# Four reorderings in a fused cross-attention and feed-forward kernel: low-rank stacks, last reciprocals, first operands, turned values

## The reference, cut to what matters

```python
x = x + xattn0(layernorm(x), ctx)      # 32 query heads of 32, 8 groups of keys and values
#   q = ln @ w_q.T ; k = ctx @ w_k.T ; v = ctx @ w_v.T ; softmax(mask(q k)) v ; @ w_out.T
x = x + ffn0(layernorm(x))
#   base = ln @ W_base.T + b_base
#   e = ln @ enc.T (rank 40) ; decoded = e @ (coefs * mask).T for 3 experts, inverse real FFT, sum, * 0.5
x = x + quantised_matmul(layernorm(x), ctx)
x = x + mixing(x)                      # 4 streams, Sinkhorn with 50 iterations
```

## Time and profile before

| | |
|---|---|
| median of 3 runs | 1081.86 us (1080.81 to 1082.34) |
| profiled execution | 1082.79 us, its span 1081.0 us |
| PE busy | 1036.2 us, 96% |
| DVE busy | 873.5 us, 81% |
| ACT busy | 663.4 us, 61% |
| mean granted TensorE clock | 0.983 of full |

### The profile page before, as it was taken

One profiled execution on the slowest core, in us unless ns is written; L12 is line 12 of the kernel. 1 busy time (PEld: TensorE's weight loads), 2 busy tenths in 40 slices (PEclk: granted clock), 3 DMA queues, 4 the chain that ended last, 5 costly groups with the idle time before them and its releaser, 6 DMA issues. The chain is left out here.

```text
span 1081.0 us, 20198 instructions
## 1 busy us (share of the span) xinstructions
PE 1036.2 (96%) x7174; PEld 782.8 (72%) x7174; DVE 873.5 (81%) x1880; ACT 663.4 (61%) x1126; POOL 93.0 (9%) x85
## 2 busy tenths in 40 slices
PE   8999999999999999999999999998999999956978
PEld 7878888777777777777777777765888887534647
DVE  5763544799999999999999999955774795879998
ACT  4332320498999889899989989942222114635837
POOL 0221011200000000000000000000003112400000
PEclk9999999999999999999999999999999999987989
DMA  8458779831133323212332321166315000000003
GB/s 330 176 162 293 258 262 277 316 116 43 39 74 73 73 68 73 52 35 63 73 73 68 73 59 33 38 240 233 118 59 170 0 0 1 1 1 1 1 1 155
DMA packets 55568, 112.95 MB, mean 104 GB/s; under 512 B 7724, under 2 KB 21164, under 8 KB 55388
## 3 DMA queue, kind: packets, MB, share of 16 engines
q1 hardware_dynamic: 55402, 112.10, 33.7%
q10 hardware_dynamic: 50, 0.16, 0.0%
q0 software_dynamic: 64, 0.00, 0.0%
HBM read 83.99 MB, written 27.26 MB: 103 GB/s over the span
## 5 line engine op out<-in xcount | busy, mean ns | idle before, releaser
L886 DVE CUSTOM_DVE_ANT_0 XS<-b_psS,b_mbias 128x1024 f32<-128x1024 f32 x256 | 310.9, 1215 | 0.9 <-PE b_psS L766 0.7
L841 ACT ACTIVATE XS<-XS,b_mins 128x1024 f32<-128x1024 f32 x256 | 295.8, 1155 | 10.1 <-DVE b_mins L886 9.5
L799 PEld LDWEIGHTS b_psT<-ident,XS 128*128 128x128 f32 x2048 | 230.0, 140 | 65.7 <-issue 47.6
L799 PE MATMUL b_psT<-ident,XS 128*128 128x128 f32 x2048 | 271.9, 276 | 1.7 <-ACT b_PT L849 1.7
L895 DVE COPY b_PT<-b_psT 128x512 f32<-128x512 f32 x256 | 176.8, 691 | 26.8 <-PE b_psT L799 24.9
L849 ACT COPY b_PT<-b_psT 128x512 f32<-128x512 f32 x256 | 149.5, 584 | 38.8 <-PE b_psT L799 30.8
L766 PE MATMUL b_psS<-XTh 128*128 128x512 f32 x512 | 155.9, 422 | 0.7 <-PEq L115 0.6
L780 PE MATMUL b_psO<-b_PT,XTh 128*32 128x256 f32 x1984 | 132.8, 385 | 0.0
L766 PEld LDWEIGHTS b_psS<-XTh 128*128 128x128 f32 x512 | 85.1, 189 | 18.5 <-DVE b_mins L886 7.7
L780 PEld LDWEIGHTS b_psO<-b_PT,XTh 128*32 128x32 f32 x1984 | 51.8, 109 | 42.1 <-issue 20.8
L416 ACT ACTIVATE a_oh<-a_psM 128x512 fp32r<-128x512 f32 x24 | 14.2, 595 | 81.4 <-PE a_psM L335 50.4
(11 more groups left out here) (268 smaller groups left out, 1616.6 us busy)
## 6 DMA issues: line engine op xcount, KB each, us to landing
XS<-in_ctx SPq DMA_DIRECT2D x16, 512.0 KB, 5.8
XTh<-QHd SPq DMA_DIRECT2D x32, 256.0 KB, 4.4
XTh<-QLd SPq DMA_DIRECT2D x32, 256.0 KB, 5.1
XS<-in_ctx_turned SPq DMA_DIRECT2D x8, 512.0 KB, 10.9
XS<-in_x SPq DMA_DIRECT2D x8, 512.0 KB, 11.4
a_wst<-in_L_xattn_w_q SPq DMA_DIRECT2D x8, 512.0 KB, 5.9
a_xn<-in_ctx_turned SPq DMA_DIRECT2D x8, 512.0 KB, 4.2
QHd<-a_oh SPq DMA_DIRECT2D x16, 256.0 KB, 5.5
```

What stands on the lines that cost most here:

```text
L799: last_t = pe.transpose(psT[:, kt, :], Pr[:, k % PR, kt * P:(kt + 1) * P], ident[:])
L841: act.activation(Pr[:, k % PR, :], Sc[:, k % 4, :], ACT.Exp, bias=mins[:, k % 4:k % 4 + 1], scale=-1.0, accum_out=sums[:, u, j:j + 1]).the ...
L886: dve.tensor_tensor_reduce(out=Sc[:, k % 4, :], in0=psS[:, k % 2, :], in1=mbias[:, qt, :], scale=1.0, scalar=3.4e38, op0=ALU.add, op1=ALU.min,
```

## The change

Four places are edited.

1. Stage A: the transposes of the values (`turn_v(0)`, `turn_v(1)`) go behind the query products 8 and 9. The first query product waits for four token tiles, the second for all eight. On DVE `keep_values` and `keep_product` of products 6 and 7 go behind the next weights' low part.
2. The seam between stages B and C: the last unit's reciprocals (DVE) and their widening (POOL) are issued in stage C, behind the barrier.
3. The first operands of stage C: the attention tile 0 is split in two parts, the first 256 columns (`FIRST` is 2 blocks of 128) ahead of the weights, the rest behind the second weight tile. The first two steps of `first_layer` wait for the first part alone.
4. The stacks of T: ACT makes T32 and its high part ahead of `std` and `attention_hi(3)`; DVE's low part goes ahead of `attention_lo(3)`; the DMA of the low rows moves from ACT's queue to SP's, ahead of the two next attention loads. DVE waits for the rest of `x` in step 2 and not in step 1.

```diff
@@ stage_a, tensor @@
-            turn_v(0)
+            pe.wait_ge(x_split, NT // 2)
             for m in range(M_Q, M_V1):
-                if m == M_Q:
-                    pe.wait_ge(x_split, NT // 2)
-                elif m == M_Q + 1:
-                    turn_v(1)
+                if m == M_Q + 1:
                     pe.wait_ge(x_split, NT)
                 product(m, XTh, XTl)
+                if m < M_Q + KVT:
+                    turn_v(m - M_Q)
@@ stage_a, vector @@
-            keep_values(0)
-            keep_product(2 * V0 + 2)
-            keep_product(2 * V0 + 3)
             for t in range(KT):
                 weights_lo(Q0 + 1 + t)
+                if t == 0:
+                    keep_values(0)
+                    keep_product(2 * V0 + 2)
+                    keep_product(2 * V0 + 3)
                 store_lo(M_Q + 2 * t)
+                ctx_lo(KT + t)
+                if t:
+                    quantise(t)
+                store_lo(M_Q + 2 * t + 1)
                 if t == 0:
                     keep_values(1)
-                ctx_lo(KT + t)
-                quantise(t)
-                store_lo(M_Q + 2 * t + 1)
+                    quantise(0)
@@ LastUnit @@
+    def spread_out(self, pool, u):
+        n = QT * HPG
+        pool.tensor_tensor(self.wide.rearrange("p t (h d) -> p (t h) d", d=DH),
+                           self.rec[:, u, :].unsqueeze(2).to_broadcast([P, n, DH]),
+                           self.one.unsqueeze(2).to_broadcast([P, n, DH]), ALU.mult).then_inc(self.rec_ready, 1)
+
+    def widen(self, pool):
+        pool.wait_ge(self.rec_ready, 2 * BG - 1)
+        self.spread_out(pool, 1)
@@ stage_b, vector @@
-            dve.wait_ge(probs, BG * STEPS)
-            end.reciprocals(dve)
@@ stage_b, gpsimd @@
-            with pool.Fori(0, BG // 2) as it:
+            with pool.Fori(0, BG // 2 - 1) as it:
                 for u in range(2):
                     widen(it, u)
+            widen(BG // 2 - 1, 0)
@@ stage_cd, sync @@
-            sp.wait_ge(wo_split, KT)
+            sp.wait_ge(wo_split, KT + 1)
...
+            sp.wait_ge(T_split, 1)
+            sp.dma_start(TS[stack_rows(1), :].bitcast(F32), lo_rows[0:RANK, 0, :].bitcast(F32)).then_inc(stacks_in, 16)
@@ stage_cd, tensor, first_layer @@
-                pe.wait_ge(op_split, 1)
                 for k in range(KT):
-                    pe.wait_ge(wo_split, k + 1)
+                    pe.wait_ge(wo_split, k + 2)
+                    if k == FIRST:
+                        pe.wait_ge(op_split, 1)
@@ stage_cd, scalar @@
-            attention_hi(0)
+            act.wait_ge(ao_in[0], 16)
+            act.activation(Lh[:, 0, 0:FIRST, :], src[:, 0, 0:FIRST * P].rearrange("p (k n) -> p k n", k=FIRST), ACT.Copy
+                           ).then_inc(wo_hi, 1)
             for k in range(KT):
                 act.wait_ge(wo_in[k // (KT // 2)], 16)
                 act.activation(WOh[:, k, :], XR[:, k, :], ACT.Copy).then_inc(wo_hi, 1)
+                if k == FIRST - 1:
+                    act.activation(Lh[:, 0, FIRST:, :], src[:, 0, FIRST * P:].rearrange("p (k n) -> p k n", k=KT - FIRST),
+                                   ACT.Copy).then_inc(op_hi, 1)
...
-                if i + 1 < NT:
+                if i + 1 < NT and i != T_TILE + 1:
                     attention_hi(i + 1)
...
-                std((i - 1) * 3 + 2)
-                if i == T_TILE + 1:
+                if i != T_TILE + 1:
+                    std((i - 1) * 3 + 2)
+                else:
                     act.wait_ge(T_done, 1)
...
-                    act.wait_ge(T_split, 1)
-                    act.dma_start(TS[stack_rows(1), :].bitcast(F32), lo_rows[0:RANK, 0, :].bitcast(F32)
-                                  ).then_inc(stacks_in, 16)
+                    std((i - 1) * 3 + 2)
+                    attention_hi(i + 1)
@@ stage_cd, vector @@
-            attention_lo(0)
+            end.reciprocals(dve)
+            lo_part(Ll[:, 0, 0:FIRST, :].rearrange("p k n -> p (k n)"), src[:, 0, 0:FIRST * P],
+                    Lh[:, 0, 0:FIRST, :].rearrange("p k n -> p (k n)"), wo_hi, 1, wo_split)
             for k in range(KT):
-                lo_part(WOl[:, k, :], XR[:, k, :], WOh[:, k, :], wo_hi, k + 1, wo_split)
+                lo_part(WOl[:, k, :], XR[:, k, :], WOh[:, k, :], wo_hi, k + 2, wo_split)
+                if k == FIRST - 1:
+                    lo_part(Ll[:, 0, FIRST:, :].rearrange("p k n -> p (k n)"), src[:, 0, FIRST * P:],
+                            Lh[:, 0, FIRST:, :].rearrange("p k n -> p (k n)"), op_hi, 1, op_split)
...
+                if i == 2:
+                    dve.wait_ge(x_in[1], 16)
                 residual(i - 1, (i - 1) % 2, 0)
-                if i == 1:
-                    dve.wait_ge(x_in[1], 16)
+                if i == T_TILE + 1:
+                    lo_part(lo_rows[0:RANK, 0, :], T32, hi_rows[0:RANK, 0, :], T_step, 3, T_split)
                 if i + 1 < NT:
                     attention_lo(i + 1)
...
-                    lo_part(lo_rows[0:RANK, 0, :], T32, hi_rows[0:RANK, 0, :], T_step, 3, T_split)
@@ stage_cd, gpsimd @@
+            end.widen(pool)
             pool.wait_ge(end.weighed, BG * 2)
```

More of the change, by code:

```diff
@@ L631, in __init__, with take @@
         self.stored = [sem(f"b_stored{u}") for u in range(2)]
-    def take(self, PT, Vs, rec, wide, sums, Os, AOs, psO):
-        self.PT, self.Vs, self.rec, self.wide, self.sums, self.Os, self.AOs, self.psO = (
-            PT, Vs, rec, wide, sums, Os, AOs, psO)
+    def take(self, PT, Vs, rec, wide, sums, Os, AOs, psO, one):
+        self.PT, self.Vs, self.rec, self.wide, self.sums, self.Os, self.AOs, self.psO, self.one = (
+            PT, Vs, rec, wide, sums, Os, AOs, psO, one)
     def weigh(self, pe, kts):
@@ L710, in stage_b @@
         psO = stack.enter_context(nc.psum_tensor("b_psO", [P, 2, S], F32))
-        end.take(PT, Vs, rec, wide, sums, Os, AOs, psO)
+        end.take(PT, Vs, rec, wide, sums, Os, AOs, psO, one)
         mbias_first = sem("b_mbias_first")
@@ L952, in widen @@
                 pool.wait_ge(rec_ready, it * 4 + (2 * u + 1))
-                pool.tensor_tensor(wide.rearrange("p t (h d) -> p (t h) d", d=DH),
-                                   rec[:, u, :].unsqueeze(2).to_broadcast([P, STEPS, DH]),
-                                   one.unsqueeze(2).to_broadcast([P, STEPS, DH]), ALU.mult).then_inc(rec_ready, 1)
-            with pool.Fori(0, BG // 2) as it:
+                end.spread_out(pool, u)
+            with pool.Fori(0, BG // 2 - 1) as it:
                 for u in range(2):
                     widen(it, u)
+            widen(BG // 2 - 1, 0)
 class EarlyLoads:
@@ L1200, in stage_cd @@
         KEEP_AT, SPREAD_AT, NORMALISE_AT = 2, 1, 4
+        FIRST = 2
         T_TILE = 1
```

## The result

The changed kernel takes 1074.91 us (median of 4 runs, 1073.35 to 1075.26), the kernel before beside it 1081.94 us. The ratio is 0.993, 95% interval 0.9914 to 0.9946. The forecast was 1074.3 us. In the experiments the same kernel ran again on another chip: 1073.0 us against 1081.44, ratio 0.9928 (0.9906 to 0.995). One execution of all that follow, the sixth of e4, took 1305.98 us at a granted clock of 0.749; it was in a slow state and is left out of the ratio.

The account below looks back on a forecast made before the run. PE, busy 96% of the span, was taken to bound the kernel up to stage E. Closing its gaps: 1.7 + 1.4 + 0.3 + 2.5 + 1.7 = 7.6 us, from 1081.9 to 1074.3 us, range 1072.3 to 1077.3.

Parts of the forecast that it names:

- Stage A: At 64 us a query product fills PE's 1.59 us wait for XTl; gain 1.6 to 1.8 us, taken as 1.7.
- the rival: SP's queue doesn't catch up and the end of stage A gives its gain back; 5.9 us gained, 1076.0 us, chance 0.12.
- Edits 2 and 3: Seam into stage C: PE's start at 712.59 moves to 711.2, 1.4 us for both together.
- the held case: Behind the seam, DVE's quarter-tile subtraction is held until POOL's widening ends at 709.55; 1.4 us gained.
- the widening then starts on POOL: Behind the seam, POOL's widening starts after DVE's reciprocals end at 708.5 and ends at 709.55.
- not held: Behind the seam, DVE's subtraction runs freely, WOl waits for WOh alone and PE starts at 711.0; 1.6 us gained.
- The wait for `x`: Stage C, tile 2: PE's 0.28 us wait goes as DVE waits for x behind the subtraction; 0.3 us gained.
- The gap ahead of `update(0)`: Stage C: T's earlier split and DMA close PE's gap, leaving 0 to about 0.3 us; gain 2.5 us.
- the two bounds of the prediction: Landing of T's low rows' DMA in stage C: at once, 745.3, or after the old 6.7 us, 752.0.
- The clock: In the 5 us behind update(0), full clock in place of 0.66 once the gap closes; gain 1.7 us.
- The sum: All gains over the whole kernel: 1.7 + 1.4 + 0.3 + 2.5 + 1.7 = 7.6 us, kept through stage E.
- Slower through stage E: PE stays at 1.2 GHz into the last mixing; 1086 us with 12 us at half clock, chance 0.03.

Follow-up runs that it names:

- e4: Kernel before with only the stacks' part: T first on ACT and DVE, low rows' DMA on SP, wait for x in step 2; 1076.81 us, ratio 0.9938.
- e1: Kernel before with only the values' transposes turned behind a query product in stage A; 1079.52 us against 1082.93, ratio 0.9969.
- e3: Kernel before with only the first operands of stage C made in parts, widening still ahead of the barrier; 1081.35 us, ratio 0.9986.
- e2: Kernel before with only the last reciprocals and widening moved behind the seam, attention tile 0 split whole; 1081.25 us, ratio 0.9982.
- e7: Changed kernel with DVE waiting for the rest of x in step 1 again; 1074.83 us, ratio 0.9915 to the kernel before.
- e5: Kernel before with three unused fp32 matmuls on PE in the gap ahead of update(0); 1080.91 us against 1081.44, ratio 0.9996.
- e6: Changed kernel with the DMA of T's low rows back on ACT's queue; 1074.02 us, ratio 0.9905 to the kernel before.
- e10: Changed kernel with three warming matmuls at the start's wait for the second key weights; 1072.51 us, ratio 0.9927 to the kernel before.
- e12: Changed kernel with five warming matmuls at the start's wait for the second key weights; 1072.77 us against 1081.77 before, ratio 0.9919.
- e8: Changed kernel with six copies on DVE ahead of Et, forcing a gap ahead of update(0); 1075.57 us, ratio 0.9949 to the kernel before.
- e9: Changed kernel with seven copies on DVE ahead of Et, forcing a gap ahead of update(0); 1076.84 us against 1083.6 before, ratio 0.9936.
- e11: Changed kernel run again unaltered on another chip; 1073.0 us against 1081.44 for the kernel before, ratio 0.9928.

## Why the prediction was right, point by point

**Stage A** was priced at 1.7 us and gives 1.79 (e1 alone 1.85). The query product starts right behind the transposes, at 64.13 with the token transposes 0.66 us later, where 63.6 was forecast. The queue catches up and the rival is out. The gain lies at the upper end of the 1.6 to 1.8 us forecast.

**Edits 2 and 3** were taken together at 1.4, the held case; 1.6 was named for the other. The traces have 1.70 from the first score to the first product, of which 1.63 lie at the seam. The step that came out otherwise is "the widening then starts on POOL": DVE's quarter began 0.09 us before POOL and was not held (0.43 us, in e3 without POOL beside it 0.42), and POOL was. So the number came near the 1.6 of "not held", but not by that mechanism. DVE was held after all, at the next instruction, the first `WOl`, and for less time. e2 has 0.72 us at the seam and e3 1.07 at the first product, together 1.79; the changed kernel has 1.63. The 0.16 us between are this hold: its first product stands 2.89 us behind the first weighing, in e3, where both `WOl` together took 2.36 us in place of 2.60, 2.73.

The Trainium skill (SBUF — State Buffer, "Who interferes with whom") calls the shared port an exclusive lock and says that issue order decides who blocks. The cases here agree, and in each the delay is about 0.14 us less than the rest of the instruction that was ahead: POOL took 1.23 for 1.04 us behind a quarter that ended 0.34 us after POOL's start, DVE 1.36 for 1.22 behind a widening that ended 0.28 us after DVE's start (e2), and the first `WOl` 1.46 for 1.22 behind a widening that ended 0.37 us after its start. The prediction drew on the right rule; which of the two came first was its error.

**The wait for `x`** was priced at 0.3 and gives 0.35; but e3 and e7 show what the sum didn't say, that without it edit 3 would have lost 0.5 us of its gain there. The parts are not independent: the sum counted 0.3 for this part, and undoing it costs 0.56. The working also has a slip here: it gains 0.3 us at tile 2, yet lets `low_product` end only 1.4 us sooner and not 1.7. With the 0.3 in it PE would have been through with tile 2 at 751.6, and the longest wait it allows for ahead of `update(0)` would have been 0.6 us, not 0.3.

**The gap ahead of `update(0)`** was 2.5 and gives 2.65, with 2.4 to 2.6 us in hand. The low rows landed 4.05 us after the DMA's issue, between the two bounds of the prediction (at once and 6.7 us). And the DMA was issued sooner than forecast. Counted from the first score, T's low part ended 4.52 us sooner than before (540.99 and 545.51), forecast were 3.75; for the rest of `x`, on which DVE waits ahead of it, came 1.46 us sooner (536.12 and 537.58), forecast were 0.7. So the slip above did no harm.

**The clock** was 1.7 and gives 1.70 in the two profiled executions; that it matches so closely is in part luck, since the kernel before happened to be profiled in an execution with the fall. The reason given, that the fall follows the gap, holds so far: it never came at that place without one (after, e4, e5, e6, e7, e10 to e12), nor behind 1.71 us (e8). Behind 2.38 to 2.52 us it came four times (before, e2, e3, e9; granted clock 0.66 to 0.68 in the 5 us behind) and behind the 2.58 of e1 it didn't. So the kernel before need not pay it in every execution, and the 1.7 us is the gain over an execution that does. What decides it at equal length stays open.

**The sum** of 7.6 us compares with 8.36 in the traces, where the start is left out. The first runs give 7.0 us by the medians and 7.6 by the ratio, with an interval of 5.8 to 9.3 us; the repeat, e11, 8.4 and 7.8, with 5.4 to 10.2. So the runs can't tell 7.0 from 8.36, and that the medians of the first runs show less isn't to be laid to an edit. The start may be what made them less: the changed kernel's first profiled execution had a start-up wait 0.73 us longer than that of before, both with a fall of the clock behind it, where e11's profile had 2.12 us and full clock. For the other three of the first runs this is inferred, since they have no trace. The prediction had no term for the start; in the fourteen profiles the last token transposes began between 59.60 and 63.54 us. That the median came out within 0.6 us of the forecast is therefore in part luck: no term was too high, the sum was 0.76 us too low against the traces, and the medians of the first runs show 1.4 us less than the traces.

The medians don't divide the gain among the edits either. Those of e1 to e4 show 3.4, 1.7, 1.6 and 6.1 us, together 12.8, half more than the whole. The traces show 1.85, 0.6, 0.45 and 4.7, together 7.6, and most of what is missing to 8.36 is the 0.5 us that edit 3 loses alone at the wait for `x`.

**Slower through stage E** did not come. From the second update on the two traces differ by 0.17 us. PE ran at half clock in stage E after as well, but DVE's iterations set the end there.

## What to carry to other kernels

Cut the trace at the same instructions of both kernels and compare the distances: start-up noise of some us drops out, and effects of 0.3 us can be read that the medians of a dozen runs don't show. Look for a second wait behind each one removed: edit 3 gains 1.07 us and keeps 0.45 until the wait for `x` behind it is moved as well. When a gap of PE is closed, read the granted clock behind it too: here it was worth 1.7 us beside the 2.65 of the gap, and it may be lost in some executions only.

## What was not expected of the hardware

- Gaps of nearly the same length did and didn't bring half clock: 2.58 us with 1.00 behind it (e1), 2.38 us with a fall (e2), 2.47 us with 0.66 and next to no transfers in it (e9).
- The wait for the second key weights at the start lasted 0.96 to 3.8 us in executions of kernels that are the same up to there.
- DVE and POOL can hold each other in turn: the quarter held the widening, and the widening, late by that, held the first `WOl`, 0.16 us at PE's first product.
- A DMA issue of 40x1024 held ACT for 1.33 us, the same issue on SP took 0.71 us.
- PE's first wait behind the barrier into stage B was 0.57 to 0.64 us in eleven profiles and 1.40 to 1.51 in three (e5, e6, e11), with the same instructions around it.
